# Moving the scan's output sums on TensorE, and their copies on ScalarE, in front of the next lot's experts in a combined scan-and-experts stage

## The chip, the cores and the metric

One core of one Trainium2 chip runs the whole kernel. The time is the device time of one execution in microseconds (us). Its engines work side by side, each through its own list of instructions in order: TensorE (PE in the profile; its weight loads are PEld), VectorE (DVE), ScalarE (ACT), GpSimd (POOL), and SyncE (SP), which issues transfers. They hand work to each other through semaphores.

## The reference

The network has four layers; the change lies in the first. There an RWKV-like attention steps a small state matrix S through time for every batch and head, and a mixture of 48 experts works on tokens that each expert picked. The two do not depend on each other:

```python
# attention of layer 0: T = 512 steps, N = 8 keys and values in a head
def step(S, inp):
    r_, w_, k_, v_, kk_, b_ = inp
    sab = jnp.einsum('bhvk,bhk->bhv', S, kk_)
    S = S * jnp.exp(w_)[:, :, None, :] + sab[..., None] * b_[:, :, None, :] + v_[..., None] * k_[:, :, None, :]
    y = jnp.einsum('bhvk,bhk->bhv', S, r_)
    return (S, y)
# experts of layer 0: E = 48, cap = 128 tokens each, S = 4 slices
xg = xf[idx]
h = jax.nn.gelu(jnp.einsum('ecd,esdm->ecsm', xg, W1) + b1[:, None], approximate=False)
y = jnp.einsum('ecsm,esmk->ecsk', h, W2) + b2[:, None]
out = jnp.zeros_like(xf).at[idx.reshape(-1)].add((y.reshape(E, cap, D) * w[..., None]).reshape(-1, D))
```

## The kernel before

`scan_and_experts_phase` does both at once. Two time steps are folded into one, so that there are 256 steps, "pairs". They are cut into 16 lots (`LOTS`) of 16 pairs, and three experts go with each lot. Each engine has a hand-written list, and the order of the calls in it is all that sets who works on what next. The work of lot n, engine by engine:

- **VectorE** runs the recurrence: eight small instructions a pair, each waiting for the one before. Its states go into the PSUM tile `rs_st`, which has two halves of eight pairs. Before VectorE writes a half again, it waits for the count `Y["hist"]`: ScalarE must have copied that half out (line 761 waits for line 786). The first half of lot n+1 needs `copy_out(n, 0)`, its second half `copy_out(n, 1)`.
- **ScalarE** has `copy_out` (line 786, states from PSUM to `hist`, which lies in `XN`), `lay_out` (line 778, turns the scan's inputs), `experts_in` (line 809 copies the turned tokens, line 815 is the Gelu), `experts_out` (line 825 scales the experts' results out of PSUM into `GX` and counts them in `X["y"]`), and `keep` (line 796, copies the finished scan outputs from PSUM; every second one also issues their transfer to DRAM, line 801). `keep(n)` counts in `Y["yev"]`.
- **GpSimd** in loop n fetches the tokens of the experts of lot n+1 (line 560), makes the products that VectorE needs for lot n+1 (lines 578, 584, 589), adds the three experts' results of lot n to DRAM (`add`, line 572, each waits for its `X["y"]`), and multiplies the copied states of lot n-1 by r (`output`, line 594, two of them, counted in `Y["out"]`). The order in the loop is fetches, first product, add 0, second and third product, add 1, output e=0, add 2, output e=1. So `output(n-1, 1)` is the last work of loop n.
- **TensorE** runs the experts of lot n (line 654 turns tokens, 659 is the first matmul, 665 and 668 the second) and `sums` (line 630): 8 fp32 matmuls that add up the products of `output` into `rs_yo`. `sums(n)` waits until both `output(n, ·)` are made, and for `keep(n-1)`, which frees `rs_yo`. Each fp32 matmul shows as two in the trace.
- **SyncE** loads expert weights and scan inputs.

What the change touches are the last two lines of TensorE's loop, and the place of `keep` in ScalarE's loop and behind it.

Of the kernel before, what the change touches and what calls it, by code (L numbers as in the profile page):

```python
# [436 lines left out]
def scan_and_experts_phase(nc, K):  # L437
# [10 lines left out]
    LOTS = M // HP  # L448
# [4 lines left out]
    with ExitStack() as ctx:  # L453
# [48 lines left out]
        def group(n):  # L502
            return range(n % TURN * EG, n % TURN * EG + EG)

        def ring(e, i):

            return (e - RING) % EL, i + (e >= RING)

        def columns(n):

            return lay[:, n // 2 % LANES, n % 2 * HP:n % 2 * HP + HP]
# [110 lines left out]
        @block.tensor  # L622
        def _(pe):
            def sums(n, rows=ALL):
                pe.wait_ge(Y["out"], 2 * (n + 1) + (rows == HIGH))
                if rows == HIGH:
                    pe.wait_ge(Y["late"], 1)
                pe.wait_ge(Y["yev"], n)
                for k in range(N):
                    last = pe.matmul(yo.rearrange("p (e m v) -> p e m v", e=2, v=N)[:, :, rows], cst("ident"), prod[:, k, :, rows],  # L630
                                     start=(k == 0), stop=(k == N - 1))
                if rows != LOW:
                    last.then_inc(Y["yo"], 1)

            pe.wait_ge(P["atf"], 1)
            pe.transpose(turnedps[:, 0, :], best[:], cst("ident")[0:R, 0:R])
            pe.transpose(turnedps[:, 1, :], atf[:], cst("ident")[0:R, 0:R]).then_inc(P["turned"], 1)
            pe.wait_ge(P["side"], 1)
            for n in range(2):
                last = pe.matmul(flips[:, n, :], cst("flip"), t[:, n, part(1)], start=True, stop=True)  # L640
            last.then_inc(P["flipped"], 1)
            pe.wait_ge(P["val"], 1)
            pe.transpose(rowsps, val[:], cst("ident")).then_inc(P["rows"], 1)
            pe.wait_ge(P["w"], 1)
            pe.transpose(colsps, w[:], cst("ident")[0:E, 0:E]).then_inc(P["cols"], 1)
            pe.wait_ge(P["wgt"], 1)
            for n in range(LOTS):
                i = n // TURN
                for e in group(n):

                    one, two = (e - 1) % EL, (e - 2) % EL
                    pe.wait_ge(X["fetched"][e], 16 * (i + 1))
                    pe.wait_ge(X["xgt"][one], i + (e >= 1))
                    pe.transpose(tps[:, 0:CAP], xg[:, e % RING, :], cst("ident")).then_inc(X["tps"][e], 1)
                    pe.wait_ge(X["xgt"][e], i + 1)
                    pe.wait_ge(X["w"][e], 48 * (i + 1))
                    pe.wait_ge(X["h"][two], i + (e >= 2))
                    for s in range(S4):
                        last = pe.matmul(hps[:, e % 2, s, :], w1[:, e, s, :], xgt[:, e % RING, :], start=True, stop=True)  # L659
                    last.then_inc(X["hps"][e], 1)  # L660
                for e in group(n):
                    pe.wait_ge(X["h"][e], i + 1)
                    pe.wait_ge(X["y"][(e - 1) % EL], i + (e >= 1))
                    out = yps[:, 0:C]
                    pe.matmul(out, cst("ones")[0:1, :], b2[0:1, e, :], start=True, stop=False,
                              skip_group_check=True)
                    for s in range(S4):
                        last = pe.matmul(out[:, 32 * s:32 * s + 32], h[:, e % EG, s, :], w2[:, e, s, :],
                                         start=False, stop=(s == S4 - 1), skip_group_check=True)
                    last.then_inc(X["yps"][e], 1)  # L670
                if n >= 2:
                    sums(n - 2)
            sums(LOTS - 2)
            sums(LOTS - 1, LOW)
            sums(LOTS - 1, HIGH)
# [93 lines left out]
        @block.scalar  # L769
        def _(act):  # L770
            def lay_out(n):

                a = n // 2 % LANES
                act.wait_ge(S["loaded"][a], 16 * USED * (n // 4 + 1))
                if n >= 4:
                    act.wait_ge(Y["out"], 2 * (n - 3))
                rows = slice(n % 2 * HP, n % 2 * HP + HP)
                act.activation(columns(n).rearrange("p m q n -> p (q n) m"), land[a][:, :, :, rows].rearrange("p q n m -> p (q n) m"),
                               ACT.Copy).then_inc(S["laid"][a], 1)

            def copy_out(n, part):

                act.wait_ge(S["full"][part], n + 1)
                if n >= 2:
                    act.wait_ge(Y["out"], 2 * (n - 1))
                act.activation(hist[:, n % 2, part * 8:part * 8 + 8].rearrange("p m v k -> p (m v k)"),  # L786
                               st[:, part].rearrange("p m v k -> p (m v k)"), ACT.Copy).then_inc(Y["hist"], 1)

            def keep(n):

                a, i = n // 2 % LANES, n // 4
                act.wait_ge(Y["yo"], n + 1)
                if n % 2 == 0:
                    act.wait_ge(S["stored"][a], 16 * i)
                for e in range(2):
                    last = act.activation(y[:, a, :, e, n % 2 * HP:n % 2 * HP + HP].rearrange("p v m -> p m v"),
                                          yo[:, e * HP * N:(e + 1) * HP * N].rearrange("p (m v) -> p m v", v=N), ACT.Copy)
                last.then_inc(Y["yev"], 1)
                if n % 2:
                    act.wait_ge(Y["yev"], n + 1)  # L800
                    act.dma_start(Yd[:, :, :, n // 2 * CP:(n // 2 + 1) * CP], y[:, a]).then_inc(S["stored"][a], 16)

            def experts_in(n):
                i = n // TURN
                for e in group(n):
                    act.wait_ge(X["tps"][e], i + 1)
                    old, times = ring(e, i)
                    act.wait_ge(X["hps"][old], times)
                    act.activation(xgt[:, e % RING, :], tps[:, 0:CAP], ACT.Copy).then_inc(X["xgt"][e], 1)
                for e in group(n):  # L810
                    act.wait_ge(X["hps"][e], i + 1)
                    act.wait_ge(X["yps"][(e - EG) % EL], i + (e >= EG))
                    for s in range(S4):
                        at = (n * EG + e % EG) * S4 + s
                        last = act.activation(h[:, e % EG, s, :], hps[:, e % 2, s, :], ACT.Gelu, bias=b1[:, at:at + 1])  # L815
                    last.then_inc(X["h"][e], 1)

            def experts_out(n):
                i = n // TURN
                for e in group(n):  # L820
                    of = n * EG + e % EG
                    act.wait_ge(X["yps"][e], i + 1)
                    old, times = ring(e, i)
                    act.wait_ge(X["added"][old], 16 * times)
                    act.activation(ye[:, e % RING, :], yps[:, 0:C], ACT.Copy, scale=WGT[:, of:of + 1]).then_inc(X["y"][e], 1)

            first_columns(act, K, slice(EARLY, 128), S["loaded"][0], range(1, USED, 2))
            act.wait_ge(P["neg"], 1)
            act.activation(w[:], rowsps, ACT.Exp, bias=small[:, 0:1], accum_out=small[:, 1:2]).then_inc(P["e"], 1)
            lay_out(0)  # L830
            lay_out(1)
            act.wait_ge(biases, 16)
            act.wait_ge(P["wgt"], 1)
            experts_in(0)
            experts_out(0)
            for n in range(LOTS):


                if n:
                    copy_out(n - 1, 1)  # L840
                if n + 2 < LOTS:
                    lay_out(n + 2)
                if n + 1 < LOTS:
                    experts_in(n + 1)
                copy_out(n, 0)
                if n >= 2:
                    keep(n - 2)
                if n + 1 < LOTS:
                    experts_out(n + 1)
            keep(LOTS - 2)  # L850
            copy_out(LOTS - 1, 1)
            keep(LOTS - 1)
            for a in range(LANES):
                act.wait_ge(S["stored"][a], 16 * (LOTS // 4))
# [3056 lines left out]
```

## Time and profile before

| | |
|---|---|
| Time, median of 3 runs | 3060.95 us (3057.07 to 3062.58) |
| Time of the profiled execution | 3063.14 us |
| Its span in the trace | 3061.4 us |
| The stage's scan, first to last step on VectorE | 367.0 to 702.6 us |
| The stage's last output copy on ScalarE | ends at 715.5 us |

A time in the trace is counted from the start of the span. "Busy" is the time in which an engine worked on data. A wait is given with the engine and tile that ended it.

### The profile page before, as it was taken

What the parts mean: (1) busy time and instruction counts of PE and PEld (TensorE: products, weight loads), DVE (VectorE), ACT (ScalarE), POOL (GpSimd) and SP (SyncE); (2) the same over time, 40 slices, a digit from 0 to 9 for tenths busy, and PEclk for the clock granted to TensorE, in tenths of its full rate; (3) what the DMA queues carried; (4) which work ended last, traced back from release to release, by engine and by line L of the source; (5) the groups of instructions that cost most, each with busy time, mean ns of one, the idle gap of its engine ahead of it and who ended that gap; (6) DMA issues with size and microseconds to landing.
All of it is one profiled execution on the core that took longest, in us unless ns stands there. A gap on an engine that the chain in (4) does not pass through costs nothing. (4 is left out here: it accounts for less than half of the span.)

```text
span 3061.4 us, 37648 instructions
## 1 busy us (share of the span) xinstructions
PE 2464.9 (81%) x10312; PEld 1075.7 (35%) x10312; DVE 2196.8 (72%) x6010; ACT 1701.7 (56%) x3079; POOL 1002.4 (33%) x971
## 2 busy tenths in 40 slices
PE   6666378875769999759999989967878888868887
PEld 2212266663343444323333333322331111224443
DVE  6999589994676655556565556668759999657776
ACT  3434344542646666452121128855569999777775
POOL 0222489981154544120000014400020000038886
PEclk8777566677879999889999999988988999989999
DMA  3112575515265665331010113300031111001110
GB/s 125 55 55 69 124 138 106 111 25 139 94 178 121 119 136 110 109 97 36 28 30 28 37 22 92 100 9 0 0 103 41 45 47 43 21 30 36 39 40 24
DMA packets 295846, 211.39 MB, mean 69 GB/s; under 512 B 155320, under 2 KB 263784, under 8 KB 295144
## 3 DMA queue, kind: packets, MB, share of 16 engines
q1 hardware_dynamic: 257696, 191.80, 23.5%
q0 software_dynamic: 19712, 14.96, 3.6%
q10 hardware_dynamic: 18256, 2.52, 0.5%
q8 instruction: 75, 1.23, 0.2%
q14 instruction: 107, 0.88, 0.1%
HBM read 136.18 MB, written 62.52 MB: 65 GB/s over the span
## 5 line engine op out<-in xcount | busy, mean ns | idle before, releaser
L2997 ACT ACTIVATE ca_pw<-ca_ps,ca_mx 128x512 f32<-128x512 f32 x512 | 342.8, 929 | 9.8 <-DVE ca_mx L3033 9.7
L2871 DVE CUSTOM_DVE_ANT_0 mx_sums<-mx_ps,w_w2f 128x512 f32<-128x512 f32 (+3 forms) x512 | 220.4, 486 | 153.2 <-PE mx_ps L2849 153.2
L3033 DVE TENSOR_REDUCE ca_mx<-ca_ps 128x1 f32<-128x512 f32 x512 | 311.6, 679 | 1.5 <-PE ca_ps L2963 1.5
L2828 PE MATMUL gm_ps<-gm_h,w_w2f 128*128 128x512 f32 x512 | 245.4, 612 | 0.0
L2997 ACT ACTIVATION_READ_ACCUMULATOR ca_pw<-ca_ps,ca_mx 128x1 f32 x512 | 229.5, 448 | 0.0
L2963 PE MATMUL ca_ps<-qs,ks 128*128 128x512 bf16 x512 | 177.0, 399 | 49.3 <-ACT ca_pw L2997 31.7
L2559 ACT ACTIVATE ta_pw<-ta_ps,w_cst 128x1280 f32<-128x1280 f32 x128 | 168.0, 1322 | 35.3 <-PE ta_ps L2440 35.0
L2903 ACT ACTIVATE gm_h<-gm_ps,w_w2f 128x512 f32<-128x512 f32 x64 | 44.0, 688 | 253.1 <-PE gm_ps L2828 253.1
L2278 ACT ACTIVATE at_pw<-at_ps 128x1280 f32<-128x1280 f32 x128 | 154.8, 1236 | 28.0 <-PE at_ps L2243 28.0
L2698 DVE TENSOR_TENSOR ta_pw<-ta_pw,w_cst 128x384 f32<-128x384 f32 x128 | 70.8, 553 | 134.8 <-ACT ta_pw L2559 132.9
L2605 POOL DMA_INDIRECT Acc<-XN,f_idx x64 | 104.5, 1633 | 157.0 <-DVE XN L2669 142.4
L2292 POOL MEMSET at_qs<- 128x1024 uint32 x4 | 3.7, 954 | 448.3 <-POOLq L36 448.3
L2974 PE MATMUL ca_o<-ca_pw,ca_vs 128*32 128x512 f32 x1024 | 138.4, 616 | 2.1 <-POOL ca_vs L3008 2.1
L761 DVE TENSOR_REDUCE rs_st<-rs_run 128x32 f32<-128x128 f32 x512 | 122.0, 284 | 11.7 <-ACT XN L786 11.7
L2963 PEld LDWEIGHTS ca_ps<-qs,ks 128*128 128x128 bf16 x512 | 40.1, 97 | 252.5 <-ACT ca_pw L2997 215.7
L3008 POOL TENSOR_TENSOR ca_vs<-VA,ca_rz 128x64 f32<-128x64 f32 x64 | 19.0, 297 | 331.9 <-DVE ca_rz L3020 331.9
L2828 PEld LDWEIGHTS gm_ps<-gm_h,w_w2f 128*128 128x128 f32 x512 | 89.3, 189 | 91.7 <-issue 91.7
L2309 DVE TENSOR_TENSOR at_pw<-at_pw,w_cb_f 128x384 f32<-128x384 f32 x128 | 70.3, 555 | 65.6 <-ACT at_pw L2278 65.5
L659 PE MATMUL ex_hps<-ex_xgt,ex_w 128*128 128x128 f32 x384 | 68.3, 332 | 47.8 <-ACT ex_h L815 25.3
L744 DVE TENSOR_TENSOR rs_run<-rs_st,rs_lay 128x96 f32<-128x96 f32 x512 | 105.7, 248 | 0.4 <-DVE rs_st L761 0.3
L2849 PE MATMUL mx_ps<-mx_ks,mx_qs 48*128 48x512 bf16 (+3 forms) x512 | 93.8, 304 | 13.7 <-DMA mx_ks<-Pd 13.7
L2301 POOL TENSOR_SCALAR_AFFINE_SELECT at_pw<-at_pw 128x128 f32<-128x128 f32 x128 | 72.8, 570 | 94.8 <-ACT at_pw L2278 94.8
(574 smaller groups left out, 6359.7 us busy)
## 6 DMA issues: line engine op xcount, KB each, us to landing
Pd<-s_p SPq DMA_DIRECT2D x64, 384.0 KB, 3.0
ex_w<-e_w SPq DMA_DIRECT2D x48, 256.0 KB
Qd<-rp_q SPq DMA_DIRECT2D x4, 2048.0 KB, 9.6
ss_ellb<-Rd SPq DMA_DIRECT2D x32, 256.0 KB, 3.4
ta_qs<-Pd SPq DMA_DIRECT2D x32, 192.0 KB
ta_ks<-Pd SPq DMA_DIRECT2D x32, 192.0 KB
GX<-Qd SPq DMA_DIRECT2D x44, 128.0 KB
SX<-Qd SPq DMA_DIRECT2D x33, 128.0 KB
```

Source lines behind the costliest of these rows:

```text
L744: v.tensor_tensor(rows(n, 0, 3, half)[:, :, :, :, 0], state(n - 1, half).unsqueeze(1).to_broadcast([128, 3, V4, N]), given(n, KK, 3), ALU. ...
L761: v.tensor_reduce(state(n, half).rearrange("p v k -> p (v k)"), rows(n, 2, 2, half).rearrange("p r v k s -> p (v k) r s"), AX.XY, ALU.add) ...
L2278: act.activation(pw[:, s % BUF, 0:SPAN], ps[:, s % 2, 0:SPAN], ACT.Exp, scale=float(1 / np.sqrt(D))).then_inc(S["power"], 1)
L2559: act.activation(pw[:, s % BUF, 0:SPAN], ps[:, s % 2, 0:SPAN], ACT.Square, scale=0.25 * 0.5 ** 0.5, bias=cst("rhalf")).then_inc(S["power"], 1)
L2605: g.indirect_dma_start(Acc, bass.IndirectOffsetOnAxis(ap=idx[:, u // 2, at:at + 1], axis=0), y[:, u % 2, c, :], None, compute_op=ALU.add). ...
L2828: last = pe.matmul(mps[:, f, :], W(("h1", "h2")[n - 2])[:, j * 512 + f * 128:j * 512 + (f + 1) * 128], src[:, j, :], start=(j == 0), stop= ...
L2849: last = pe.matmul(ps[:, u, at:at + n], qs[:, g, h % GH, jq * 128:(jq + 1) * 128], ks[:, g, h % GH, 0:n], start=True, stop=True)
L2871: last = v.tensor_tensor_reduce(out=sums[:, u, at:at + n], in0=ps[:, u, at:at + n], in1=K["w2f"]("down")[:, T - n:T], scale=-1.0, scalar=3 ...
L2963: pe.matmul(ps[:, q % BANKS, :], ks[:, G % 2, h % GH, jk * 128:(jk + 1) * 128], qs[:, G % 2, h % GH, :], start=True, stop=True).then_inc(S ...
L2974: last = pe.matmul(O[32 * a:32 * a + M, G % 2, :], vs[:, h % BUF, jk, :], pw[:, h % BUF, jk, :], start=False, stop=(a == GH - 1 and jk == ...
L2997: act.activation(pw[:, h % BUF, jk, :], ps[:, (h * NB + jk) % BANKS, :], ACT.Exp, bias=mx[:, h % H, jk:jk + 1], accum_out=z[:, h % H, jk:j ...
L3033: v.tensor_reduce(mx[:, h % H, jk:jk + 1], ps[:, q % BANKS, :], AX.X, ALU.max, negate=True).then_inc(S["top"], 1)
```

## The change

On TensorE `sums(n - 2)` stands ahead of the experts of lot n and no longer behind them. On ScalarE `keep(n - 2)` stands ahead of `experts_in(n + 1)` and no longer behind `copy_out(n, 0)`. After the loop, the last copy of states stands ahead of `keep(LOTS - 2)`. No instruction is added or taken away.

```diff
             for n in range(LOTS):
+
+                if n >= 2:
+                    sums(n - 2)
                 i = n // TURN
                 for e in group(n):
...
                     last.then_inc(X["yps"][e], 1)
-                if n >= 2:
-                    sums(n - 2)
             sums(LOTS - 2)
             sums(LOTS - 1, LOW)
...
                 if n + 2 < LOTS:
                     lay_out(n + 2)
+                if n >= 2:
+                    keep(n - 2)
                 if n + 1 < LOTS:
                     experts_in(n + 1)
                 copy_out(n, 0)
-                if n >= 2:
-                    keep(n - 2)
                 if n + 1 < LOTS:
                     experts_out(n + 1)
+            copy_out(LOTS - 1, 1)
             keep(LOTS - 2)
-            copy_out(LOTS - 1, 1)
             keep(LOTS - 1)
```

TensorE's list before, around the first group of sums (`ex_tps` is the turn, `ex_hps` the first matmul, `ex_yps` the second, `rs_yo` the scan's sums; the semaphore `ex_h8` is the one that expert 8, the last of lot 2, counts when its Gelu is done; other semaphores bear names left from an earlier stage):

```order
L665 MATMUL ex_yps<-ex_b2,w_cst 128x128 [waits ex_y7,ex_h8]
L668 MATMUL ex_yps<-ex_w2,ex_h 128x32 x4
L630 MATMUL rs_yo<-XN,w_cst 128x256 [waits opx_x4,opx_x1]
L630 MATMUL rs_yo<-XN,w_cst 128x256 x7
L654 MATMUL ex_tps<-w_cst,ex_xg 128x128 [waits rp_stored01,rp_k20]
L659 MATMUL ex_hps<-ex_xgt,ex_w1 128x128 [waits ex_h7,rp_w0,rp_stored10]
L659 MATMUL ex_hps<-ex_xgt,ex_w1 128x128 x3
```

After, around the first group of sums again, which now follows expert 5, the last of lot 1:

```order
L668 MATMUL ex_yps<-ex_b2,w_cst 128x128 [waits ex_y4,ex_h5]
L671 MATMUL ex_yps<-ex_w2,ex_h 128x32 x4
L630 MATMUL rs_yo<-XN,w_cst 128x256 [waits opx_x4,opx_x1]
L630 MATMUL rs_yo<-XN,w_cst 128x256 x7
L657 MATMUL ex_tps<-w_cst,ex_xg 128x128 [waits rp_q0,rp_f11]
L662 MATMUL ex_hps<-ex_xgt,ex_w1 128x128 [waits ex_h4,rp_ez1,rp_q1]
L662 MATMUL ex_hps<-ex_xgt,ex_w1 128x128 x3
```

The first sums have moved up by three experts, and so have all others: `sums(n-1)`, which stood behind the experts of lot n+1, stands ahead of them.

ScalarE's list before, from `lay_out(4)` in the pass n=2 to the next `lay_out`:

```order
L778 ACTIVATE rs_lay<-SX 128x88x16
L809 ACTIVATE ex_xgt<-ex_tps 128x128 x3
L815 ACTIVATE ex_h<-ex_hps,ex_b 128x128 x12
L786 ACTIVATE XN<-rs_st 128x512
L796 ACTIVATE rs_y<-rs_yo 128x16x8 x2
L825 ACTIVATE GX<-ex_yps,WGT 128x128 x3
L786 ACTIVATE XN<-rs_st 128x512
L778 ACTIVATE rs_lay<-SX 128x88x16
```

And after:

```order
L779 ACTIVATE rs_lay<-SX 128x88x16
L797 ACTIVATE rs_y<-rs_yo 128x16x8 x2
L810 ACTIVATE ex_xgt<-ex_tps 128x128 x3
L816 ACTIVATE ex_h<-ex_hps,ex_b 128x128 x12
L787 ACTIVATE XN<-rs_st 128x512
L826 ACTIVATE GX<-ex_yps,WGT 128x128 x3
L787 ACTIVATE XN<-rs_st 128x512
L779 ACTIVATE rs_lay<-SX 128x88x16
```

The two copies of scan outputs (`rs_y`) have moved from between the experts' two halves to a place ahead of both.

## Rows read from the trace of the kernel before

**Rows 1.** The page: busy us, share of the span, instructions.
```profile
PE 2464.9 (81%) x10312; PEld 1075.7 (35%) x10312; DVE 2196.8 (72%) x6010; ACT 1701.7 (56%) x3079; POOL 1002.4 (33%) x971
```

**Rows 2.** Busy time by stretch: PE, PEld, DVE, ACT, POOL, granted TensorE clock, DMA.
```profile
402.00:423.00 21.00, 13.70 (x54) 11.52 (x54) 20.88 (x136) 9.51 (x21) 19.03 (x12) 0.50 0.81 142
...
444.00:465.00 21.00, 17.39 (x74) 14.66 (x74) 20.88 (x134) 10.18 (x23) 19.44 (x12) 0.66 0.86 149
```

**Rows 3.** Waits of 353 to 720 us: total, times, longest.
```profile
DVE rs_st L761 <- ACT XN L786: 11.7, 6, 9.7
```

**Rows 4.** Timeline of DVE: start, us; first steps of lots 14 and 15.
```profile
661.60 0.42 DVE L744 TENSOR_TENSOR rs_run<-rs_st,rs_lay 128x96 f32<-128x96 f32 x2
...
681.78 0.42 DVE L744 TENSOR_TENSOR rs_run<-rs_st,rs_lay 128x96 f32<-128x96 f32 x2
```

**Rows 5.** Timeline of POOL: an add after a wait, and the last outputs of loops 1 to 14.
```profile
379.73 1.64 POOL L572 DMA_INDIRECT Acc<-GX,IDX  x1 [8.62 <-ACT GX L825]
...
410.29 2.96 POOL L594 TENSOR_TENSOR XN<-XN,rs_lay 128x1024 f32<-128x1024 f32 x1
...
455.31 2.95 POOL L594 TENSOR_TENSOR XN<-XN,rs_lay 128x1024 f32<-128x1024 f32 x1
458.42 1.01 POOL L560 DMA_INDIRECT ex_xg<-Xt,IDX  x1 [0.16 <-issue]
...
464.14 1.63 POOL L572 DMA_INDIRECT Acc<-GX,IDX  x1 [0.17 <-issue]
...
475.68 2.96 POOL L594 TENSOR_TENSOR XN<-XN,rs_lay 128x1024 f32<-128x1024 f32 x1
...
680.75 2.96 POOL L594 TENSOR_TENSOR XN<-XN,rs_lay 128x1024 f32<-128x1024 f32 x1
```

**Rows 6.** Timeline of PE: sums of lots 0 and 2, the turns that follow.
```profile
424.52 6.60 PE L630 MATMUL rs_yo<-XN,w_cst 128*128 128x256 f32 x16
...
449.35 0.27 PE L654 MATMUL ex_tps<-w_cst,ex_xg 128*128 128x128 f32 x1
...
465.40 4.95 PE L630 MATMUL rs_yo<-XN,w_cst 128*128 128x256 f32 x16
470.19 0.27 PE L654 MATMUL ex_tps<-w_cst,ex_xg 128*128 128x128 f32 x1
```

**Rows 7.** Groups by form of PE, 353 to 720 us: busy, mean ns.
```profile
L630 PE MATMUL rs_yo<-XN,w_cst 128*128 128x256 f32 x240 | 80.0, 506 | 4.9 <-POOL XN L594 4.9
```

**Rows 8.** Timeline of ACT, from the token copy of lot 2 on.
```profile
378.53 0.37 ACT L825 ACTIVATE GX<-ex_yps,WGT 128x128 f32<-128x128 f32 x1 [1.42 <-PE ex_yps L668]
...
406.89 0.41 ACT L809 ACTIVATE ex_xgt<-ex_tps 128x128 f32<-128x128 f32 x1
...
418.44 0.37 ACT L825 ACTIVATE GX<-ex_yps,WGT 128x128 f32<-128x128 f32 x1 [0.94 <-PE ex_yps L668]
...
457.49 0.62 ACT L786 ACTIVATE XN<-rs_st 128x512 f32<-128x512 f32 x1
...
459.32 0.37 ACT L825 ACTIVATE GX<-ex_yps,WGT 128x128 f32<-128x128 f32 x1 [0.71 <-PE ex_yps L668]
...
465.63 0.37 ACT L825 ACTIVATE GX<-ex_yps,WGT 128x128 f32<-128x128 f32 x1 [2.79 <-PE ex_yps L668]
465.90 0.59 ACT L786 ACTIVATE XN<-rs_st 128x512 f32<-128x512 f32 x1
466.37 3.66 ACT L778 ACTIVATE rs_lay<-GX 128x1408 f32<-128x1408 f32 x1
...
478.27 0.38 ACT L825 ACTIVATE GX<-ex_yps,WGT 128x128 f32<-128x128 f32 x1
...
484.59 0.37 ACT L825 ACTIVATE GX<-ex_yps,WGT 128x128 f32<-128x128 f32 x1 [2.79 <-issue]
```

**Rows 9.** Timeline of the stage's end: POOL, PE, ACT.
```profile
695.62 4.67 POOL L594 TENSOR_TENSOR XN<-XN,rs_lay 128x1024 f32<-128x1024 f32 x2 [11.90 <-PE rs_yo L630]
...
705.75 3.17 POOL L594 TENSOR_TENSOR XN<-XN,rs_lay 128x512 f32<-128x512 f32 x2 [3.72 <-PE rs_yo L630]
...
710.11 1.86 POOL L594 TENSOR_TENSOR XN<-XN,rs_lay 128x512 f32<-128x512 f32 x1
...
700.35 5.25 PE L630 MATMUL rs_yo<-XN,w_cst 128*128 128x256 f32 x16 [4.87 <-POOL XN L594]
...
714.90 0.60 ACT L796 ACTIVATE rs_y<-rs_yo 128x128 f32<-128x128 f32 x2 [8.23 <-PE rs_yo L630]
```

## The prediction

> **What bounds the kernel now.** The page [rows 1] gives TensorE the largest share, but the change lies in one stage, so I read the stage by stretches first. Within 444 to 465 us [rows 2] VectorE is busy 20.88 of 21 us, GpSimd 19.44, TensorE 17.39, ScalarE 10.18. The reader is to see two engines without slack. VectorE's lot takes 681.78 - 661.60 = 20.18 us [rows 4]. GpSimd's loop takes 478.64 - 458.26 = 20.38 us, from the end of one loop's last output to the end of the next (455.31 + 2.95 and 475.68 + 2.96 [rows 5]), with nothing but gaps of 0.2 to 0.3 us in it. The list of waits says what VectorE still loses to ScalarE's copies of states: 11.7 us in 6 waits, 9.7 of it in one at lot 1 [rows 3]. So the stage runs at the pace of VectorE and GpSimd, with TensorE and ScalarE filling in behind.
>
> What keeps it so is slack between the engines. GpSimd wants the first result of the experts (add 0) at 464.14 [rows 5]. ScalarE delivered it at 459.32 + 0.37 = 459.69 [rows 8], 4.45 us ahead. That the experts of this lot could begin at 449.35 [rows 6], 8.9 us before GpSimd ended its loop at 458.26, is what buys this.
>
> **The change part by part.**
>
> *Sums ahead of the experts.* `sums(n-1)` needs `output(n-1, 1)`, the last work of GpSimd's loop n. Now it stands ahead of the experts of lot n+1, and a matmul list is followed in order, so these experts wait for the end of that loop. Call that end T(n). Queued behind the waiting sums are the turn, both matmuls and thus every step of `experts_in` and `experts_out` of lot n+1. Who waits for them: `copy_out(n, 0)`, behind `experts_in(n+1)` on ScalarE, and behind it VectorE; and on GpSimd `add(n+1, 0)`, which stands in loop n+1 ahead of the second product, of both other adds and of the outputs. The last of these outputs, `output(n, 1)`, releases the next sums. This closes a ring, one turn of it per lot. It was open before, because experts did not wait for outputs. One turn is:
>
> - Sums. 80.0 us for 15 of them [rows 7] is 5.33 each; single ones are 4.95 and 6.60 [rows 6]. The sums now begin after an idle engine, so I take 5.5.
> - From the first turn of the lot to the end of the first result's copy: 459.69 - 449.35 = 10.34 and 478.65 - 470.19 = 8.46 [rows 6, 8]. I take the mean, 9.4. `keep` no longer stands in this path, which is worth some tenths in the lots where its transfer was issued.
> - From that copy's end to the add on a GpSimd that waits: 379.73 - (378.53 + 0.37) = 0.8 [rows 5, 8].
> - GpSimd from add 0 to the end of output e=1: 478.64 - 464.14 = 14.5 [rows 5].
> - From there to the sums: 700.35 against 695.62 + 4.67, so 0.1 [rows 9].
>
> The sum is 30.3 us per lot against 20.38. A second way to the same number: add 0 stood 464.14 - 458.26 = 5.9 after T, and can now not stand before 5.5 + 9.4 + 0.8 + 0.1 = 15.8 after it, so each loop gains 9.9 us of waiting.
>
> How many turns: T(1) is 410.29 + 2.96 = 413.25, and nothing ahead of it is touched. T(14), the last loop with an output, is 680.75 + 2.96 = 683.71 [rows 5]. There are 13 turns between. New T(14) = 413.25 + 13 × 30.3 = 807.2, which is 123.4 later.
>
> *Does another engine need more than 30.3?* ScalarE: its last expert copy ends 466.00 - 449.35 = 16.65 or 484.96 - 470.19 = 14.77 after the first turn [rows 6, 8], so at T + 22.3 at most. `copy_out(n, 1)` is then done at T + 22.9. GpSimd wants it for `output(n, 0)` at T + 15.8 + 7.4 (475.68 less the 4.14 between the two outputs is 471.54, which is 7.4 behind add 0). That is T + 23.2, just enough. VectorE: `copy_out(n, 0)`, 8.14 behind the first turn (457.49 [rows 8]), is done at T + 14.4. It then has 30.3 us for a lot of 20.18. It loses some 10 us in each lot from the second on, where it lost 2.0 in 14 before.
>
> *`keep` ahead of `experts_in`.* It costs what it did (two small copies). But `sums(n-1)` waits for `keep(n-2)`, which now stands behind `copy_out(n-1, 1)` and the `lay_out` of 3.66 us. That makes a second ring: sums 5.5, experts to the last copy 15.7 (mean of 16.65 and 14.77), copy of states 0.5 and `lay_out` 3.7 (465.90 to 470.03 [rows 8]), `keep` about 0.6 (as the last one, 0.60 [rows 9]), together 26.0. It is shorter than 30.3, so it is hidden in GpSimd's ring and costs nothing as long as that holds. Without that cover it would still cost 26.0 - 20.4 = 5.6 a lot.
>
> *The end.* Before, the last `keep` ended at 714.90 + 0.60 = 715.50, which is T(14) + 31.8. Now TensorE ends sums and experts of lot 15 at T + 21.3, ScalarE's `copy_out(14, 1)` is done at T + 21.9, GpSimd's last two whole outputs take 4.67 and sums(14) 5.25 [rows 9], which is T + 32.0. From the low output at 705.75 to the end were 9.75. This makes T + 41.8, 10.0 more than before. The last copy of states ahead of `keep(14)` yields nothing: VectorE ends its last lot by T + 14.4 + 20.2 = T + 34.6, and its copy (0.6) is wanted 4.36 behind the low output (710.11 - 705.75), at T + 36.4.
>
> *The sum.* 123.4 + 10.0 = +133 us, on the profiled execution's 3063.14 us makes 3196.5. The median of the runs is 2.2 lower, so 3194. For the bounds: with the shortest rows (4.95 + 8.46 + 0.4 + 14.5 + 0.1 = 28.4) 13 turns give 98.8, with 8 at the end +107, 3168. With all of TensorE's work at the low clock, below, +191.
>
> **The clock of TensorE.** In 402 to 423 us, where TensorE was busy 13.7 of 21 us, the granted clock stayed at 0.50 (1.2 GHz) throughout; in 444 to 465, with 17.4 busy, it was 0.66 on average [rows 2]. The new ring keeps it busy about 17 of 30 us with a hole of some 8 in each, less than in either. Against a low clock speaks that the sums are one solid piece: the 4.95 us of sums at 465.40 is shorter than the 6.60 us at 424.52 [rows 6], so the clock rises inside such a piece, and the experts right behind it profit. I take the same mix as before.
>
> The Trainium skill, page "TensorE: Matmul & The Clock Gate", section "HAM oscillation — how this bites in real kernels", says that waits between short bursts send the array back to the low clock, so that each burst starts slowly. By that rule each lot's sums start at 1.2 GHz after the hole, and if they are too short to lift it, all experts follow at 1.2 GHz. It speaks against this change beyond the waiting alone. The time it would give is that of rival 1.
>
> **The rivals.**
>
> 1. *TensorE stays at the low clock for whole lots.* The sums are then 6.60, and the experts take 12.4 to the first result (406.89 less 0.45 for the turn, to 418.44 + 0.37 [rows 8]). The turn of the ring is 6.6 + 12.4 + 0.8 + 14.8 + 0.1 = 34.7, 13 of them 451.1, T(14) 180.6 later, with 10 at the end +191: 3252. For it: the stretch at 402 [rows 2]. Against: the solid piece of sums.
> 2. *Only the ring over `keep` and `lay_out` counts*, because GpSimd gets its adds in time. Then 26.0 per lot, 13 × 26.0 - 270.5 = 67.5, and 10 at the end: +78, 3139. Against it: the first result came 459.69 - 458.26 = 1.4 after T and comes 15.8 after it, 14.4 later against a slack of 4.45.
> 3. *The delay is paid once.* GpSimd catches up, and only the end of the stage lies later: +10, 3071. Against it: its loop is 20.38 long at VectorE's 20.18 [rows 4, 5], so it has nothing to catch up with.
> 4. *Not slower.* If the outputs were made before TensorE is through with the previous lot's experts, the sums would start at once and `keep` would be out of the way of `experts_out`; VectorE's five small waits (11.7 - 9.7 = 2.0 us [rows 3]) would go: 3059. It decides at T being no later than the end of the experts before, which is at most 449.35 less the shortest sums of 4.95, 444.4 [rows 6]. T is 458.26, 13.9 us too late, and each further turn of the ring keeps it late.
>
> **How the numbers follow.** The ring of 30.3: 0.74. Rival 1, whole or in most lots: 0.16. Rival 2: 0.05. Rival 3: 0.03. Rival 4: 0.02. The likeliest gives 3194; its own range is 3168 to 3225. The range for 8 in 10 takes in rival 1 nearly whole: 3165 to 3250. A change of 0.2%, 6 us, is about what a measurement of this kernel can tell from none. Faster by more: 0.01. Within: 0.02. Slower by more: 0.97.
>
> **What would show it.** In the changed profile the stage should end near 849 us (807.2 + 41.8) and not at 715.5. VectorE's wait for ScalarE's copy (line 761) should be about 140 us in some 14 waits of 10. GpSimd's adds should wait about 10 us per lot for ScalarE's expert copy. TensorE should sit idle about 8 us ahead of each group of sums, ended by GpSimd's output. The starts of sums should lie 30 us apart. Right at the clock: 0.6 to 0.75 in the stretches; at 0.50 throughout it is rival 1. If GpSimd's adds do not wait, the ring is not closed and the prediction is wrong. A spacing of 26 would name rival 2.

## The result and the profile after

The changed kernel takes 3198.01 us in the median of 4 runs (3175.52 to 3200.93), the kernel before 3061.32 (4 runs). The ratio is 1.0433, with a 95% interval of 1.0385 to 1.0482: 137 us slower. The profiled execution took 3196.91 us, its span is 3195.2 us against 3061.4 before, 133.8 more. The stage's last output copy ends at 851.21 us against 715.50, 135.7 more, so the whole loss lies in this stage.

The list of waits of the changed kernel, 353 to 860 us (total, times, longest; its lines are one to three further on than before):

```profile
ACT ex_xgt L810 <- PE ex_tps L657: 198.7, 46, 13.8
DVE rs_st L762 <- ACT XN L787: 153.7, 15, 11.1
...
POOL Acc L572 <- ACT GX L826: 144.2, 15, 10.5
PE rs_yo L630 <- POOL XN L594: 143.8, 17, 10.7
```

The same waits in the kernel before, 353 to 720 us:

```profile
ACT ex_xgt L809 <- PE ex_tps L654: 64.0, 45, 4.4
...
PE rs_yo L630 <- POOL XN L594: 8.7, 3, 4.9
POOL Acc L572 <- ACT GX L825: 8.6, 1, 8.6
```

Read it as a ring. TensorE's sums wait for GpSimd's outputs, ScalarE's token copies wait for TensorE's turns behind these sums, GpSimd's adds wait for ScalarE's expert copies. The three waits have grown by 135.1, 134.7 and 135.6 us, some ten in each lot, and the stage by 135.7. VectorE hangs off it: its wait for copied states was 11.7 us in 6 waits [rows 3] and is 153.7 in 15, 142.0 more. That all four engines now wait, each for another and each for about the same time, is what a ring looks like; behind one slow engine I would expect that engine to have no waits.

One turn of it in the timeline of GpSimd:

```profile
563.51 2.95 POOL L594 TENSOR_TENSOR XN<-XN,rs_lay 128x1024 f32<-128x1024 f32 x1
566.62 1.01 POOL L560 DMA_INDIRECT ex_xg<-Xt,IDX  x1 [0.16 <-issue]
...
570.19 1.97 POOL L578 TENSOR_TENSOR rs_run<-rs_lay 128x1024 f32<-128x1024 f32 x1
581.12 1.63 POOL L572 DMA_INDIRECT Acc<-GX,IDX  x1 [8.96 <-ACT GX L826]
...
588.50 2.94 POOL L594 TENSOR_TENSOR XN<-XN,rs_lay 128x1024 f32<-128x1024 f32 x1
591.59 1.59 POOL L572 DMA_INDIRECT Acc<-GX,IDX  x1 [0.16 <-issue]
592.62 2.94 POOL L594 TENSOR_TENSOR XN<-XN,rs_lay 128x1024 f32<-128x1024 f32 x1
```

of TensorE:

```profile
566.52 5.88 PE L630 MATMUL rs_yo<-XN,w_cst 128*128 128x256 f32 x16 [9.41 <-POOL XN L594]
572.24 0.27 PE L657 MATMUL ex_tps<-w_cst,ex_xg 128*128 128x128 f32 x1
...
595.62 6.68 PE L630 MATMUL rs_yo<-XN,w_cst 128*128 128x256 f32 x16 [9.97 <-POOL XN L594]
```

and of ScalarE (the first expert result):

```profile
579.93 0.39 ACT L826 ACTIVATE GX<-ex_yps,WGT 128x128 f32<-128x128 f32 x1
```

The output ends at 566.46, the sums begin 0.06 later, the turn stands at 572.24, the first expert result is copied at 580.32, the add begins 0.8 later, and the next pair of outputs ends at 595.56. That is 29.1 us. Most lots take 30.6, since the clock of TensorE falls earlier in them. Read in steps of 1 us, the granted clock here is 0.50 until 570 us, rises to 1.00 while the sums run, and is back at 0.50 from 582 on, behind the first expert's result. In the lot whose sums begin at 809.32 it is back at 0.50 from 821 on, ahead of that result, which is copied 9.82 us after the turn (814.82 to 824.64) and not 8.08. By stretches (columns as in [rows 2]):

```profile
444.00:474.00 30.00, 17.86 (x73) 14.86 (x73) 19.51 (x125) 10.09 (x23) 18.35 (x11) 0.61 0.34 63
490.00:520.00 30.00, 17.75 (x73) 14.88 (x73) 19.49 (x125) 9.73 (x22) 18.91 (x11) 0.61 0.24 47
```

30 us now hold about what 21 us held [rows 2], and VectorE and GpSimd, which had no slack, idle more than a third of the time.

GpSimd's last outputs of loops 1 and 14, and the stage's end on it and on ScalarE, from the timeline:

```profile
410.35 2.95 POOL L594 TENSOR_TENSOR XN<-XN,rs_lay 128x1024 f32<-128x1024 f32 x1
...
806.32 2.95 POOL L594 TENSOR_TENSOR XN<-XN,rs_lay 128x1024 f32<-128x1024 f32 x1
831.51 4.68 POOL L594 TENSOR_TENSOR XN<-XN,rs_lay 128x1024 f32<-128x1024 f32 x2 [22.24 <-ACT XN L787]
...
850.61 0.60 ACT L797 ACTIVATE rs_y<-rs_yo 128x128 f32<-128x128 f32 x2 [6.83 <-PE rs_yo L630]
```

Between the first and the last of the loops' outputs are 395.97 us for 13 lots, 30.46 each (809.27 - 413.30), against 270.46, 20.80 each, before [rows 5]. From there to the end are 41.9 us against 31.8.

### The profile page after: what moved, and what is told of

It is laid out like the page before. It is cut to its first block and busy times, and to the rows that moved or that the text cites. A ratio compares the mean times of both kernels' runs of the same rounds, so it can differ in the third digit from the quotient of the medians.

```text
span 3195.2 us, 37557 instructions
## 1 busy us (share of the span) xinstructions
PE 2458.9 (77%) x10221; PEld 1083.3 (34%) x10312; DVE 2196.2 (69%) x6010; ACT 1700.1 (53%) x3079; POOL 1000.7 (31%) x971
## 5 line engine op out<-in xcount | busy, mean ns | idle before, releaser
L762 DVE TENSOR_REDUCE rs_st<-rs_run 128x32 f32<-128x128 f32 x512 | 122.0, 283 | 153.7 <-ACT XN L787 153.7
L2964 PE MATMUL ca_ps<-qs,ks 128*128 128x512 bf16 x482 | 167.3, 396 | 53.3 <-ACT ca_pw L2998 35.4
L630 PE MATMUL rs_yo<-XN,w_cst 128*128 128x256 f32 (+1 forms) x272 | 89.8, 504 | 143.8 <-POOL XN L594 143.8
L572 POOL DMA_INDIRECT Acc<-GX,IDX x48 | 76.9, 1602 | 153.7 <-ACT GX L826 144.2
L630 PEld LDWEIGHTS rs_yo<-XN,w_cst 128*128 128x128 f32 x272 | 69.6, 271 | 160.2 <-POOL XN L594 146.4
L810 ACT ACTIVATE ex_xgt<-ex_tps 128x128 f32<-128x128 f32 x48 | 13.5, 282 | 198.7 <-PE ex_tps L657 198.7
```

The costliest lines, as they stand in the source:

```text
L572: g.indirect_dma_start(Acc, bass.IndirectOffsetOnAxis(ap=IDX[:, of:of + 1], axis=0), ye[:, e % RING, :], None, compute_op=ALU.add).then_in ...
L762: v.tensor_reduce(state(n, half).rearrange("p v k -> p (v k)"), rows(n, 2, 2, half).rearrange("p r v k s -> p (v k) r s"), AX.XY, ALU.add) ...
L2964: pe.matmul(ps[:, q % BANKS, :], ks[:, G % 2, h % GH, jk * 128:(jk + 1) * 128], qs[:, G % 2, h % GH, :], start=True, stop=True).then_inc(S ...
```

## The experiments

Every time below is a median, beside that of the kernel before measured along with it, since the latter moved between 3057.7 and 3064.7 us.

### The parts alone

The sums' move alone can't stand. `sums(n-1)` would wait for `keep(n-2)`, which in ScalarE's old order comes behind token copies that wait for TensorE behind these sums. That is a deadlock by the lists, and was not tried. The other two parts can.

`keep` ahead of the experts, on ScalarE alone:

```diff
+                if n >= 2:
+                    keep(n - 2)
                 if n + 1 < LOTS:
                     experts_in(n + 1)
                 copy_out(n, 0)
-                if n >= 2:
-                    keep(n - 2)
```

> The kernel before with one part of the change alone: on ScalarE keep(n-2) stands ahead of experts_in(n+1); TensorE's order is the old one. Theory (the ring over GpSimd's last output and its adds makes the loss, and it needs the sums ahead of the experts): the ring stays open, so almost nothing of the 137 us. keep now waits for sums(n-2), which TensorE runs while ScalarE lays out, and delays the first token copy by some 0.3 to 0.6 us a lot: 3061 to 3070 us, likeliest 3065. Rival (keep behind the copy of states and lay_out closes a ring of its own, 26 us a lot): 3061 + 14 x 5.6, some 3139 us.

3058.82 us against 3058.03, ratio 1.0002 (0.9992 to 1.0011). Not even the few microseconds that I gave it show. ScalarE waits in `keep` (19.6 us in 3 waits in the kernel before) instead of in the token copy that follows (64.0 in 45 before), says its list of waits (total, times, longest):

```profile
ACT ex_xgt L809 <- PE ex_tps L654: 49.0, 32, 2.4
...
ACT rs_y L796 <- PE rs_yo L630: 37.4, 16, 8.3
...
DVE rs_st L761 <- ACT XN L786: 12.3, 6, 9.9
```

The last copy first:

```diff
+            copy_out(LOTS - 1, 1)
             keep(LOTS - 2)
-            copy_out(LOTS - 1, 1)
             keep(LOTS - 1)
```

> The kernel before with only the last part of the change: behind the loop, the last copy of states stands ahead of keep(14). Theory: the copy starts 3 us earlier, but the last products wait for sums(14) and come 4.4 us after that anyway, so no change, 3061 us within 1. Rival (the last states are on the path that ends the stage): 3 us less, 3058 us.

3059.70 us against 3058.03, ratio 1.0003 (0.9994 to 1.0013). The copy starts at 702.48 and not at 706.03, but GpSimd's low outputs stand at 705.57 as before, because they wait for sums(14), and the end stays (715.34 against 715.50). From the timeline of GpSimd:

```profile
705.57 3.23 POOL L594 TENSOR_TENSOR XN<-XN,rs_lay 128x512 f32<-128x512 f32 x2 [3.73 <-PE rs_yo L630]
```

So the loss is the sums' move, with the `keep` that it needs.

### The changed kernel again

> The changed kernel once more, on the chip and beside the runs of the other kernels of this call, since its first runs lay between 3175 and 3201 us. Theory: the lot takes 29.1 to 30.7 us, depending on how the rises of TensorE's clock fall on the sums and the experts; 3175 to 3201 again, so that differences below 15 us to after_copies say nothing about a ring. Rival (one run of four was an accident): all runs within 3195 to 3201.

3197.66 us (3179.42 to 3206.16) against 3064.65, ratio 1.0450 (1.0433 to 1.0468). The spread is real. The profiled execution here has a span of 3177.7 us, and its sums alternate in the timeline of TensorE:

```profile
582.00 5.21 PE L630 MATMUL rs_yo<-XN,w_cst 128*128 128x256 f32 x16 [10.40 <-POOL XN L594]
610.44 6.33 PE L630 MATMUL rs_yo<-XN,w_cst 128*128 128x256 f32 x16 [9.39 <-POOL XN L594]
640.04 5.20 PE L630 MATMUL rs_yo<-XN,w_cst 128*128 128x256 f32 x16 [10.42 <-POOL XN L594]
```

Two lots take 58.0 us, 29.0 each. In the slower execution above most take 30.6. The waits of the ring are the same; what differs is the clock. From the first to the last sums of the steady lots the granted clock is 0.68 on average here (408 to 784 us) and 0.62 there (413 to 809 us). In both lots shown, the first expert's result is out before the clock falls (at about 595 and 626 us).

### Shortening the ring at GpSimd

The second product and the sum of products go into the time in which add 0 waits:

```diff
                 first_product(n + 1)
-                add(n, 0)
                 second_product(n + 1)
                 both_products(n + 1)
+                add(n, 0)
                 add(n, 1)
```

> The changed kernel, but GpSimd makes the second product and the sum of products of lot n+1 ahead of add(n,0), in the time in which that add waits. Theory: this takes 5.1 us out of the ring over the add, which falls from 30.6 to 25.4; but the outputs then wait for copy_out(n,1), which is only 2.0 to 2.6 us ahead of them now, so that the next ring, over the copy, takes over at some 28.6: 13 x 2.0, 3172 us. Rival (the adds' ring is not what sets the pace, TensorE's clock is): 3198 us. Had the ring over the add no other behind it: 3132 us.

3165.28 us against 3058.03, ratio 1.0357 (1.0339 to 1.0375). A lot takes 28.5 us, from the sums at 411.72 to those at 782.21. This is the number forecast, but not for the reason forecast, so it is in part luck. The work behind the add is in the ring, or the gain would be nil, and something takes its place, or the gain would be 5.1 a lot. I had named the copy of states. The list of waits says otherwise:

```profile
POOL Acc L572 <- DMA Acc<-GX,IDX: 32.1, 11, 4.4
...
POOL XN L594 <- ACT XN L787: 21.7, 5, 20.2
```

Of the outputs' waits for copied states one of 20.2 us lies at the end of the stage (22.2 in the changed kernel), which leaves 1.5 us in 4 lots. But add 1 could not follow add 0 at once: it stands at 604.81, 5.26 us behind add 0 at 599.55, where 6.32 lay between them with both products in the gap (581.12 to 587.44). It waits for the second expert's result or for the transfer of add 0 to land, whichever comes later.

### Earlier states, alone and with it

```diff
-                if n:
-                    copy_out(n - 1, 1)
                 if n + 2 < LOTS:
                     lay_out(n + 2)
...
                 copy_out(n, 0)
+                copy_out(n, 1)
                 if n + 1 < LOTS:
                     experts_out(n + 1)
-            copy_out(LOTS - 1, 1)
             keep(LOTS - 2)
```

> The changed kernel, but ScalarE's copy_out(n,1) stands between experts_in(n+1) and experts_out(n+1), and no longer behind both, so GpSimd's outputs get their states some 7 us earlier. Theory (the ring runs through add(n+1,0), which waits for the first expert result): the outputs were not waiting for states, so nothing is gained; the copy of 0.5 us now stands ahead of the first result, 0 to 0.5 us a lot more: 3198 to 3205 us, GpSimd's adds still wait 9 to 10 us each lot. Rival (the ring runs through the copy of states, the adds only wait in its shadow): up to 2 us a lot less, 3172 us or less.

3183.51 us against 3058.03, ratio 1.0406 (1.0389 to 1.0424). GpSimd's adds wait for ScalarE 15 times and 140.5 us, as without the edit (144.2), so it is the same ring. But the median lies 14 us under that of the changed kernel, where I expected 0 to 7 more. Its lots take 30.1 us. The changed kernel by itself has turns of 29.0 to 30.6, and the granted clock here is 0.65 on average (412 to 804 us), between its 0.62 and 0.68. So I hold this for another mix of clocks; that fits, but no run shows it apart.

With the products' edit as well:

> The changed kernel with both edits: GpSimd's products ahead of add(n,0), and ScalarE's copy_out(n,1) between the two halves of the experts. Theory: either edit alone leaves the other's ring; together both get shorter, and what is left goes over the second and third expert result: 25.4 to 27.5 us a lot, 3130 to 3158, likeliest 3144 us. Rival (the pace of the lots is set by TensorE's low clock or by the place of the sums as such): within 5 us of 3198.

3170.32 us against 3058.27, ratio 1.0362 (1.0347 to 1.0377). A miss: no better than the products' edit alone, where 3144 was expected. So the copy of states was not what held that kernel at 28.5. GpSimd's waits in this kernel:

```profile
POOL Acc L572 <- ACT GX L826: 63.3, 15, 5.0
POOL Acc L572 <- DMA Acc<-GX,IDX: 45.7, 21, 3.8
```

and adds 0 and 1 of one lot in its timeline:

```profile
600.28 1.64 POOL L572 DMA_INDIRECT Acc<-GX,IDX  x1 [4.60 <-ACT GX L826]
604.53 1.59 POOL L572 DMA_INDIRECT Acc<-GX,IDX  x1 [2.62 <-DMA Acc<-GX,IDX]
```

`add(n, 1)` also waits until the transfer of `add(n, 0)` has landed, 4.25 us after its issue. In the old order the products stood between the two and hid this. I had counted an add at its 1.1 us of issue.

### Taking the adds out of the ring

```diff
                 first_product(n + 1)
+                if n:
+                    output(n - 1, 0)
+                    output(n - 1, 1)
                 add(n, 0)
                 second_product(n + 1)
                 both_products(n + 1)
                 add(n, 1)
-                if n:
-                    output(n - 1, 0)
                 add(n, 2)
-                if n:
-                    output(n - 1, 1)
```

> The changed kernel, but both outputs of lot n-1 stand ahead of add(n,0) in GpSimd's loop, so that sums(n-1) no longer waits for an add of the experts of lot n. Theory: the ring over the adds is gone; left is sums, experts, copy_out(n,1) behind them, two outputs: 20.1 to 22.2 from the end of an output to the end of that copy plus 5.4, so 25.5 to 27.6 a lot, 3130 to 3158 us, likeliest 3151. Rival (the add is not in the ring): 3198.

3138.64 us against 3058.27, ratio 1.0265 (1.0250 to 1.0280). Expected were 3130 to 3158. The adds' waits for ScalarE are no longer among the long ones; the outputs now wait for the copied states, 56.4 us in 15 waits, and a lot takes 26.1 us (sums at 406.27 to 771.04, 14 lots). The control, the same order of GpSimd in the kernel before:

> The kernel before, with GpSimd's order of after_outputs alone: both outputs of lot n-1 ahead of add(n,0), adds 1 and 2 next to each other. Theory: add 2 then waits some 3 us for the transfer of add 1 to land, GpSimd's loop grows from 20.4 to about 22.7 us and sets the pace: 14 x 2.3, about 32 us above the kernel before in the same call. Rival (GpSimd has that time to spare): within 6 us of before.

3088.89 us against 3057.67, ratio 1.0108 (1.0091 to 1.0125): 31 us, as forecast. Adds 1 and 2 in its timeline:

```profile
577.68 1.60 POOL L572 DMA_INDIRECT Acc<-GX,IDX  x1 [0.15 <-issue]
582.71 1.57 POOL L572 DMA_INDIRECT Acc<-GX,IDX  x1 [3.43 <-issue]
```

and a line of its waits:

```profile
DVE rs_run L743 <- POOL rs_run L589: 40.6, 13, 5.2
```

Add 2 stands still for 3.4 us behind add 1. The profile names no releaser here; by the program it waits for add 1 to land. And VectorE, which never waited for GpSimd's products in a steady lot before, waits for them 13 times.

Now adds and states together:

> The changed kernel with the outputs ahead of the adds in GpSimd's loop and copy_out(n,1) between the two halves of the experts. The sums stay ahead of the experts. Theory: no ring is left that is longer than a lot of VectorE or GpSimd (from output to output: sums 5.7, first half of the experts 8, two copies 1.1, two outputs 4.8, together 19.6 against 20.4), so nearly all of the 137 us comes back: 3060 to 3080 us, likeliest 3068. Rival (sums ahead of the experts cost by themselves, by TensorE's idle time and low clock): well above 3100 us.

3109.06 us against 3058.27, ratio 1.0166 (1.0151 to 1.0180). Better by 30 than the outputs' edit alone and by 74 than the states' alone, and still 41 above the 3068 expected. What is left has its own line in the list of waits:

```profile
PE rs_yo L629 <- ACT rs_y L796: 64.1, 15, 7.5
```

and ScalarE's timeline shows what stands ahead of the copy that TensorE waits for:

```profile
596.34 3.66 ACT L778 ACTIVATE rs_lay<-GX 128x1408 f32<-128x1408 f32 x1
599.71 0.74 ACT L796 ACTIVATE rs_y<-rs_yo 128x128 f32<-128x128 f32 x2
```

The sums at 600.59 wait for `keep` behind `lay_out`. It is the second ring of the prediction, the one costed at 26.0 us. My expectation for this run had left it out. The sums here stand 24.5 to 25.8 us apart, 24.9 on average (401.41 to 699.99, 12 lots). Those 12 lots at 4.1 us more than the 20.8 before are 49 of the 51 us that this kernel loses. The 31 us of the control do not come on top: GpSimd's outputs wait for ScalarE's copies 14 times (26.9 us in the same list), so its own order is not what sets the pace here.

### Is `keep` part of the loss as things stand?

In the changed kernel, `keep(n-1)` between the experts' halves in place of `keep(n-2)` ahead of both:

```diff
-                if n >= 2:
-                    keep(n - 2)
                 if n + 1 < LOTS:
                     experts_in(n + 1)
                 copy_out(n, 0)
+                if n:
+                    keep(n - 1)
                 if n + 1 < LOTS:
                     experts_out(n + 1)
             copy_out(LOTS - 1, 1)
-            keep(LOTS - 2)
             keep(LOTS - 1)
```

> The changed kernel, but with keep(n-1) between the two halves of the experts on ScalarE in place of keep(n-2) ahead of both, so that sums never wait for a keep behind lay_out. Theory: the ring over keep is 24 to 26 us and lies in the shadow of the ring over the adds (30.6), so taking it away changes nothing: 3198 us, within the spread of the changed kernel's own runs (3175 to 3206). Rival (keep's place is part of the loss): 3175 us or less in the median.

3199.78 us (3194.98 to 3201.50) against 3057.67, ratio 1.0470 (1.0453 to 1.0488). Nothing gained: the ring of 26 is hidden in that of 30.5, and the waits are those of the changed kernel:

```profile
POOL Acc L572 <- ACT GX L826: 145.7, 15, 10.7
PE rs_yo L630 <- POOL XN L594: 143.2, 17, 10.6
```

### All rings opened, the sums still in front

This is the states' edit, the later `keep`, and GpSimd's order with the adds kept apart:

```diff
                 first_product(n + 1)
+                if n:
+                    output(n - 1, 0)
+                    output(n - 1, 1)
                 add(n, 0)
                 second_product(n + 1)
-                both_products(n + 1)
                 add(n, 1)
-                if n:
-                    output(n - 1, 0)
+                both_products(n + 1)
                 add(n, 2)
-                if n:
-                    output(n - 1, 1)
```

> The changed kernel with every ring opened, the sums still ahead of the experts: GpSimd makes both outputs ahead of the adds and keeps the adds apart by a product each; ScalarE's copy_out(n,1) stands between the halves of the experts; and keep(n-1), not keep(n-2), stands there too, right behind the sums that it follows. Theory: what was left in after_outputs_copies were the ring over keep behind lay_out (24.3 us a lot, 15 waits of TensorE for ScalarE, 64 us) and adds that wait for the previous one's transfer. With both gone the lot falls to what one engine needs, 20.4 to 21.2 us: 3060 to 3078 us, likeliest 3068. Rival (TensorE idle before the sums and its clock cost some us a lot by themselves): the lot stays at 22 us or more, 3085 us or more.

3068.31 us against 3064.65, ratio 1.0011 (1.0000 to 1.0022). 129 of the 133 us that the changed kernel lost beside it are back, with the sums in front of the experts. Two groups of sums in the timeline of TensorE:

```profile
592.62 6.34 PE L629 MATMUL rs_yo<-XN,w_cst 128*128 128x256 f32 x16
...
614.36 5.70 PE L629 MATMUL rs_yo<-XN,w_cst 128*128 128x256 f32 x16
```

and the last expert's copy on ScalarE:

```profile
592.71 0.37 ACT L825 ACTIVATE GX<-ex_yps,WGT 128x128 f32<-128x128 f32 x1 [2.79 <-PE ex_yps L670]
```

No wait stands ahead of these sums, which begin as the last expert's matmuls end (the last result's copy is at 592.71). They stand 21.3 us apart on average (401.20 to 699.58, 14 lots), where a lot took 20.8. It does not beat the kernel before.

### The wait that the kernel before still had

`copy_out(n, 0)` ahead of `experts_in(n+1)` and `copy_out(n, 1)` behind it, in the kernel before:

```diff
-                if n:
-                    copy_out(n - 1, 1)
                 if n + 2 < LOTS:
                     lay_out(n + 2)
+                copy_out(n, 0)
                 if n + 1 < LOTS:
                     experts_in(n + 1)
-                copy_out(n, 0)
+                copy_out(n, 1)
                 if n >= 2:
                     keep(n - 2)
...
             keep(LOTS - 2)
-            copy_out(LOTS - 1, 1)
             keep(LOTS - 1)
```

> The kernel before, with copy_out(n,0) ahead of experts_in(n+1) and copy_out(n,1) between the two halves of the experts. It aims at VectorE's wait of 9.7 us in lot 1 and the five small ones (11.7 us in all). Theory: the waits go, but GpSimd's loop of 20.38 us is longer than VectorE's lot and takes part of it back: 3050 to 3058 us, likeliest 3054. Rival (the copies ahead of the experts delay TensorE's experts, which are as slow as a lot at 20.4 us): 3061 or more.

3061.69 us against 3058.27, ratio 1.0010 (1.0000 to 1.0020). The wait of 9.7 us is gone, and nothing was gained, where 4 us were expected. From the list of waits:

```profile
DVE XN L767 <- PE rs_yo L630: 8.3, 1, 8.3
...
DVE rs_run L744 <- POOL rs_run L589: 5.9, 8, 1.7
...
DVE rs_st L761 <- ACT XN L786: 2.8, 3, 1.3
```

and one from that of the kernel before:

```profile
DVE XN L767 <- ACT XN L786: 4.1, 1, 4.1
```

VectorE is early by what it saved, then waits 5.9 us in 8 waits for GpSimd's products, and 8.3 us at the end for sums(14), where its last wait was 4.1. Sums(14) begin at 699.88 and not at 700.35. So GpSimd's loop of 20.4 us sets the end; in the kernel before, VectorE had lain behind GpSimd by its wait in lot 1, which hid that. The rival of the expectation, experts delayed by the copies, would have moved these sums later.

## Why the prediction was right

It gave 3194 us, and 3198 were measured. The ring was found from the lists and its terms from the rows. Term by term:

- *Sums.* 5.5 taken, 85.7 us for 15 measured, 5.71 each. From their start to the turn are 5.72 in the lot shown and 5.50 in the last (809.32 to 814.82). They begin at the low clock, and it rises while they run.
- *First turn to the first result's copy.* 9.4 taken, as the mean of a quick and a slow row; 8.08 in the lot shown, up to 9.8 in others (814.82 to 824.64). What the other terms leave of 30.46 is about 9.5.
- *Copy to add* 0.8, measured 0.8. *Add to last output* 14.5, measured 14.44. *Output to sums* 0.1, measured 0.06.
- *The turn* 30.3, measured 30.46 on average; T(14) 807.2, measured 809.27.
- *The end* 41.8 behind T(14), measured 41.9. Here two small misses cancel: the low output begins at T + 33.0 (842.25) and not at 32.0, and 8.96 us lie from there to the end and not 9.75. The sum +133, measured +133.8 between the profiled executions.
- *VectorE.* Forecast were 140 us in 14 waits; 153.7 in 15 are those and the 9.7 of lot 1, which was left where it was.
- *TensorE idle ahead of the sums.* Forecast 8, measured 9.4 to 10.7, as its experts were through at T + 21.3 or sooner; the forecast had counted to ScalarE's last expert copy, at T + 22.3.

Four small things in it do not stand as written, and none changes the forecast. The lower bound's 0.4 from copy to add, and its 8 at the end, come from no row. Rival 1 takes 14.8 for GpSimd's part, where the row gives 14.5. Rival 2 sets the copy's end at 1.4 against the add's start at 15.8; end to end it is 1.4 against 15.0. And T + 21.3 is the end of ScalarE's last expert copy, not of TensorE's work. Some luck is in how near the median came: whether an execution turns at 29.0 or at 30.6 us was not forecast, and that decides between about 3175 and 3200.

*Rival 1*, TensorE at 1.2 GHz for whole lots, did not come. The granted clock is 0.61 on average in 444 to 474 us and 0.66 in 580 to 610. So it is at 2.4 GHz for a part of the time, though 9 us of idleness stand ahead of each group of sums. The Trainium skill, page "TensorE: Matmul & The Clock Gate", section "HAM oscillation — how this bites in real kernels", says that a wait between short bursts sends the array back to the low clock, so that the next burst starts there. The trace agrees: the granted clock is 0.50 when the sums begin, at 566.52 and at 809.32. It is 1.00 before they end, so the experts behind them run fast at first. The spread between 3175 and 3206 us goes with how long that lasts: 0.62 on average in an execution of 3197 us, 0.68 in one of 3179.

*Rival 2*, the ring over `keep`, was rightly put in the shadow (later_keep changes nothing), and came out when the longer ring was opened (24.9 us a lot in after_outputs_copies). *Rival 3*, a delay paid once, is out: the waits come in each of the lots. *Rival 4* did not come either: the sums waited 9.4 us or more for GpSimd's outputs in each of these lots.

What I had wrong stands in the expectations, not in the prediction: an add was counted at its issue, and the wait for the landing of the one before was left out (after_products, after_products_copies), and the `keep` ring was forgotten for after_outputs_copies. That these misses did not touch the prediction is because in the changed kernel products stand between the adds.

The change is slow by the lists it was paired with, not by the place of the sums: with GpSimd's outputs first, the states copied earlier and `keep` moved behind its own sums, the same place costs 4 us, at the edge of what can be told. That is the sum of all four edits: the kernel before with the other three alone was not run.

## What to carry to other kernels

Before a piece of work is moved ahead of another in an engine's list, write down what it waits for and walk on from what now stands behind it, engine by engine, until the walk ends or comes back. If it comes back one lot later, the pace is the length of the walk and not the busiest engine: count it in rows and multiply by the lots. Opening the longest ring uncovers the next one (30.5, 28.5, 26.1, then 24.9 us here), so list them all first. And removing a wait of an engine gains nothing when another engine's loop is as long (before_copies).

## What the runs showed of the hardware

A scattering add to DRAM issued by GpSimd takes about 1.1 us until its next work begins (581.12 to 582.21), but the next add, when it must wait for the first to land, starts 4.25 us after it (600.28 to 604.53 in after_products_copies), and up to 5.0 in before_outputs_first (577.68 to 582.71). From these figures I estimate that two such adds need 3 to 4 us of other work between them.

GpSimd's output of 128x1024 elements shows 2.94 us right behind the issue of an indirect transfer, and two in a row without one 4.68 us, 2.34 each, with VectorE busy in both cases. Most of the difference is overlap in the rows: the output at 588.50 begins 0.54 us before the row of the transfer ahead of it ends (587.44 + 1.60), and takes 2.40 from there.

The same kernel had a turn of 29.0 us in one execution and of 30.6 in another, at a granted clock of 0.68 and 0.62 on average. The changed kernel, whose ring passes through matmuls, is less steady than the kernel before: 3175 to 3206 us against 3053 to 3073.
